# Both normalisations of the mixing stage on ScalarE, with a shift from GpSimd, in place of VectorE

## The chip, the core and the metric

The kernel runs on one core of a Trainium2 chip. The metric is the device time of one execution in microseconds (us). The engines are PE (TensorE: PE is its matmuls, PEld its weight loads), DVE (VectorE), ACT (ScalarE), POOL (GpSimd) and SP (SyncE, which issues DMAs). They run their own instruction streams and meet at semaphores.

## The reference

One transformer-like block over 8 batches of 512 tokens with 256 features, all in float32; a class row is put ahead of each batch.

```python
h = _L0_tok_ref(x, w_qkv, b_qkv, w_out, b_out)            # attention, 16 heads
h = concatenate([broadcast(cls_tok), h], axis=1)           # 513 rows
h = h + _L0_attn_ref(_layernorm(h), a_params, B_w, C_w, D) # linear recurrence over the tokens, + D * u
h = h + _L0_ffn_ref(_layernorm(h), ...)                    # shared expert + top 2 of 8 experts

def _layernorm(x, axis=-1, eps=1e-05):
    m = jnp.mean(x, axis=axis, keepdims=True)
    v = jnp.var(x, axis=axis, keepdims=True)
    return (x - m) / jnp.sqrt(v + eps)
```

The two calls of `_layernorm` are what the change is about. In the recurrence's input they give `u`, in the experts' input `u2`.

## The kernel before

The program has three stages. The first makes queries, keys and values and runs attention for all batches (to about 505 us of the span). The second, `stage_mix`, which this case is about, takes the batches one by one. The third (from about 790 us) runs tiles of 128 token rows through the experts that were chosen.

A batch is four tiles (TT = 4) of 128 tokens on the partitions by 256 features. The mixing stage has nine steps, b = 0 to 8, written out by hand (`batches`, which calls each engine's `step`). Step b carries batch b through the recurrence (`this`), batch b-1 through the shared expert (`prev`), and batch b+1 through its output projection and first normalisation (`nxt`). What an engine does, in what order, is fixed by the order of the calls in its `step`; only semaphores (`ev[...]`) couple the engines.

Around the change one batch goes so:

- PE turns (transposes) the second-normalised rows `u2` (`turn_rows`, L1210), ACT copies the result to `u2_short`, DVE makes the rest (`cut_second`), ACT copies `u2_T`, PE makes the router's logits (L1347) and the first part of the shared expert's products (L73). Meanwhile PE projects the next batch's heads, and DVE adds the bias and takes the statistics (`first_sum`: `sum_and_statistics`, L1429 to L1437).
- POOL raises variance + eps of the four tiles to the power -1/2 (`inverse_deviation`, L1069). DVE makes `u` of the next batch: `normalise`, L1443, four instructions, (row - mean) * inverse deviation. DVE adds the router's bias (L1560), ACT takes the sigmoid (L1187), DVE chooses two experts (L854 to L1501) and multiplies the shared expert's gates (L1415).
- PE turns `u`, ACT copies the result to `u_T` behind a silu (L1132, L1136), PE makes the state's input (`make_state`, L1243), DVE turns and scans it (`turn_back`, L1477 on; `make_hidden`), PE makes `y` (L1255).
- POOL computes d * u + h (L1081, L1084) as soon as `u` is there and the choice of the batch before is made.
- DVE adds `y` and takes the second statistics, POOL the power, DVE places the rows' slots (`place`, L1460 to L1466), makes `u2` (L1443 again) and adds the shared expert's result (L1420). Meanwhile PE runs `shared_down` (L1281). POOL issues eight indirect DMAs of slots a batch (L1103); the next batch's power stands behind the sixth.

In steps 1 to 5 ACT also rounds one early weight (L891) and DVE subtracts it (`cut_weights`, L899), between the gates and `turn_back`. In batch 0 the attention stage's code makes `u` (`beside`), and in step 0 DVE carries the class rows as well.

ACT keeps one set of function tables at a time. Sigmoid and silu lie in different sets, so an ACT_TABLE_LOAD stands ahead of each of the two; the plain copies need none.

Of the kernel before, what the change touches and what calls it, by code (L numbers as in the profile page):

```python
# [23 lines left out]
FP32 = mybir.dt.float32  # L24
# [3 lines left out]
ALU = mybir.AluOpType  # L28
ACT = mybir.ActivationFunctionType
# [891 lines left out]
def stage_mix(nc, mem, dram):  # L921

    ident = mem["ident"]
    with ExitStack() as ctx:
# [22 lines left out]
        w_s_rest, w_s = mem["w_s_rest"], (mem["wg_s"], mem["wu_s"])  # L947
        stats = sb("mix_stats", [P, TT, 6], FP32)
        mv = sb("mix_mv", [P, TT, 2], FP32)
        rstd = sb("mix_rstd", [P, TT], FP32)  # L950
        probs = sb("mix_probs", [P, TT, E], FP32)
        for name, shape in (("counts", [P, E]), ("need", [P, E]), ("ends", [P, E]), ("tile_f", [P, 2, TILES])):
            mem[name] = sb(name, shape, FP32)
# [111 lines left out]
        @block.gpsimd  # L1065
        def _(pool):
            def inverse_deviation(b, which):
                pool.wait_ge(ev[f"stats{which}"], b + 1)
                pool.tensor_tensor(rstd[:, :], mv[:, :, 1], mem["minus_half"][:, 0:TT], ALU.pow).then_inc(ev[f"pow{which}"], 1)  # L1069

            def step(b, par, prev, this, nxt):
                if this:
# [55 lines left out]
        def _(act):  # L1128
# [9 lines left out]
            def class_copy(n, to, bank):  # L1138

                act.wait_ge(ev["cls_turned"], n + 1)  # L1140
                act.activation(to, cls_ps[bank][:, 0:D].rearrange("p (c n) -> p c n", c=2), ACT.Copy).then_inc(ev["cls_copied"], 1)

            def step(b, par, prev, this, nxt):
                if this and prev:
                    copy_turned(u_T, b, "u_turned", "uT_copied")
# [26 lines left out]
                if last:  # L1172
                    act.wait_ge(ev["y_made"], 2 * B)
                    for n in (10, 11, 12):
                        shorten_weights(act, mem, n)
                if last:
                    copy_turned(u2_T, b, "u2_turned", "u2T_copied")
                    act.wait_ge(ev["u2T_copied"], b + 1)
                    act.activation(short(u2_short[:, :, :]), u2_T[:, :, :], ACT.Copy).then_inc(ev["shared_shortened"], 1)
                elif this:  # L1180
                    copy_turned(short(u2_short), b, "u2_turned", "shared_shortened")

                    act.wait_ge(ev["u2_cut"], b + 1)
                    copy_turned(u2_T, b, "u2_turned", "u2T_copied")
                if this:
                    act.wait_ge(ev["logits_biased"], b + 1)
                    act.activation(probs[:, :, :], probs[:, :, :], ACT.Sigmoid).then_inc(ev["sigmoid"], 1)  # L1187
                    silu(b, 0)
# [222 lines left out]
        def _(dve):  # L1411
# [11 lines left out]
            def sum_and_statistics(b, rows, term, which, link):  # L1423

                product, done = (("out_made", "h_done"), ("y_made", "h2_done"))[which - 1]
                for n in range(2):
                    dve.wait_ge(ev[product], 2 * b + n + 1)
                    pair = rows[:, 2 * n:2 * n + 2, :]
                    dve.tensor_tensor(pair, made[:, n, :].rearrange("p (t n) -> p t n", t=2),  # L1429
                                      pair if term is None else term, ALU.add).then_inc(ev[done], 1)  # L1430
                    dve.wait_ge(ev[done], 2 * b + n + 1)
                    for t in (2 * n, 2 * n + 1):
                        link(dve.bn_stats(stats[:, t, :], rows[:, t, :]), wait=(t == TT - 1))  # L1433
                dve.sem_inc(ev["stats_ready"])
                for t in range(TT):
                    link(dve.bn_aggr(mv[:, t, :], stats[:, t, :]), wait=(t == TT - 1))
                dve.tensor_scalar(mv[:, :, 1], mv[:, :, 1], EPS, None, ALU.add).then_inc(ev[f"stats{which}"], 1)  # L1437

            def normalise(b, rows, which):
                dve.wait_ge(ev[f"pow{which}"], b + 1)  # L1440
                to = (u, u2)[which - 1]
                for t in range(TT):
                    last = dve.tensor_scalar(to[:, t, :], rows[:, t, :], mv[:, t, 0:1], rstd[:, t:t + 1],  # L1443
                                             ALU.subtract, ALU.mult)
                last.then_inc(ev["u_done" if which == 1 else "u2_done"], 1)

            def cut_second(b):
                dve.wait_ge(ev["shared_shortened"], 2 + b + 1)
# [47 lines left out]
            def step(b, par, prev, this, nxt):  # L1496
# [32 lines left out]
                    class_act()  # L1529
                elif nxt:  # L1530
                    place(b - 1, 1 - par)
                if this:
                    dve.wait_ge(ev["u2_turned"], b)
                    dve.wait_ge(ev["u2_stored"], 16 * b)
                    normalise(b, h2[:, par, :, :], 2)
                if this and not nxt:
                    place(b - 1, 1 - par)
                if prev:
# [13 lines left out]
                    first_sum(b + 1)  # L1552
                if not prev:
                    class_add()
                if nxt:
                    dve.wait_ge(ev["u_turned"], b + 1)
                    normalise(b + 1, h, 1)
                if this:
                    dve.wait_ge(ev["logits_made"], b + 1)
                    dve.tensor_tensor(probs[:, :, :], turn[:, 0, 0:TT * E].rearrange("p (t e) -> p t e", e=E),  # L1560
# [38 lines left out]
            def beside(g, n):  # L1599
# [8 lines left out]
                if (g, n) == (2, 0):  # L1608
                    copy_turned(heads_T, "heads_turned", "hT_copied")
                    class_state()  # L1610
                    first_sum(0)
                elif (g, n) == (2, 1):
                    normalise(0, h, 1)
                elif (g, n) == (3, 0):
                    copy_turned(u_T, "u_turned", "uT_copied")
                    class_end()
                    turn_back(0, scan)
                elif (g, n) == (3, 1):
                    make_hidden(0, scan)
# [519 lines left out]
```

## Time and profile before

| | us |
|---|---|
| median of 3 runs | 1169.42 (1168.76 to 1169.72) |
| the profiled execution | 1169.99 |
| its span | 1168.3 |
| PE busy | 1112.9 (95%) |
| DVE busy | 916.5 (78%) |
| ACT busy | 584.5 (50%) |
| POOL busy | 401.2 (34%) |

The span runs from the first to the last instruction that the profiler saw; the execution's time is a little longer. The busy shares are means over all three stages. In the mixing stage batches 1 to 6 follow each other in steady steps of about 34.95 us. In a timeline row stand the start and the length in us, engine, line, operation, the tile written <- the tiles read, and in brackets how long the engine had been idle and what ended that.

### The profile page before, as it was taken

The numbers are of one execution on the slowest core, as the hardware profiler recorded it, in microseconds if no ns is written. First come the engines' busy times: TensorE is split into PE (matmuls) and PEld (weight loads), VectorE is DVE, ScalarE is ACT, GpSimd is POOL, SyncE is SP. The second block draws the span as 40 slices with busy tenths as digits, with TensorE's granted clock in tenths as the row PEclk, the third lists the DMA queues.
The fourth block names the chain that finished last, engine by engine and source line by source line (L and its number), as shares of the span: only waits on it lengthen the run. The fifth ranks groups of instructions, "written<-read, shape, count | busy, mean of one in ns | idle before, by whom it ended". The sixth has DMA issues, their size and how long they took to land.

```text
span 1168.3 us, 22138 instructions
## 1 busy us (share of the span) xinstructions
PE 1112.9 (95%) x6022; PEld 713.9 (61%) x6023; DVE 916.5 (78%) x1567; ACT 584.5 (50%) x973; POOL 401.2 (34%) x516
## 2 busy tenths in 40 slices
PE   6998999999999999989999999977999999999996
PEld 3654333333333333477777777766888888888885
DVE  3788888888888888678888888786777777777775
ACT  3544777777777777641332322532444444444442
POOL 3011630101011111203455343453555555545553
PEclk9998999999999999999999999988999999999998
DMA  8786232323323332041345431222333333333332
GB/s 290 262 259 220 67 110 70 107 72 103 94 82 97 95 83 70 19 142 39 91 109 109 92 81 52 48 57 63 58 50 53 52 55 54 54 54 54 54 55 33
DMA packets 108691, 105.38 MB, mean 90 GB/s; under 512 B 42464, under 2 KB 97904, under 8 KB 108624
## 3 DMA queue, kind: packets, MB, share of 16 engines
q1 hardware_dynamic: 90528, 81.18, 24.3%
q0 software_dynamic: 18112, 23.57, 11.6%
q8 instruction: 25, 0.41, 0.2%
q14 instruction: 26, 0.21, 0.1%
HBM read 64.88 MB, written 39.68 MB: 89 GB/s over the span
## 4 chain that ended last, share of the span: by engine, by line
PE 70%; DVE 10%; POOL 5%; issue 4%; DMA 1%; ACT 1%; POOLq 0%; DVEq 0%; SPq 0%; ACTq 0%
PE mix_pairs L73 20%; PE pv L673 11%; PE by_key L662 10%; PE by_query L653 9%; PE mix_made L1821 9%; POOL kept_table L1103 4%; PE mix_turn L1808 3%; PE mix_made L1255 2%; PE mix_made L1243 2%; PE by_query L694 2%; PE mix_turn L1788 1%; DVE mix_stats L1433 1%; DVE k_mix_u L1443 1%; DVE mix_h L1429 1%; DVE mix_back L1486 1%
## 5 line engine op out<-in xcount | busy, mean ns | idle before, releaser
L747 DVE TENSOR_REDUCE k_neg_max<-by_query 128x2 f32<-128x1024 f32 x240 | 282.8, 1220 | 49.0 <-PE by_query L653 46.2
L807 ACT ACTIVATE k_wu_e<-by_key 128x512 f32<-128x512 f32 x512 | 270.2, 600 | 65.5 <-PE by_key L662 65.4
L662 PE MATMUL by_key<-k_wg_e 99*128 99x512 bf16 x512 | 175.2, 384 | 3.4 <-DVE pv L783 3.0
L1765 POOL DMA_INDIRECT out_rows<-x_y,k_slot x72 | 114.0, 1583 | 158.3 <-PE mix_turn L1788 111.6
L653 PE MATMUL by_query<-k_wg_e 96*128 96x512 bf16 x480 | 144.7, 382 | 0.0
L1863 ACT ACTIVATE x_gate<-mix_pairs 128x512 f32<-128x512 f32 x72 | 43.0, 597 | 200.8 <-PE mix_pairs L73 200.8
L673 PE MATMUL pv<-k_wu_e,k_wd_e 128*17 128x512 f32 x1024 | 134.6, 598 | 0.2 <-ACT k_wu_e L807 0.2
L73 PE MATMUL mix_pairs<-w_short,x_T 128*128 x288 | 121.7, 423 | 2.1 <-issue 2.1
L1821 PEld LDWEIGHTS mix_made<-x_wd,x_acts_T 128*128 128x128 f32 x864 | 111.2, 188 | 7.4 <-ACT x_acts_T L1886 0.9
L73 PE MATMUL mix_pairs<-w_short,x_rest 128*128 x288 | 114.6, 398 | 0.0
L1821 PE MATMUL mix_made<-x_wd,x_acts_T 128*128 128x256 f32 x864 | 112.6, 279 | 0.7 <-ACT x_acts_T L1886 0.7
L1928 DVE TENSOR_TENSOR x_wd<-k_wd_e,x_wd 128x1024 fp32r<-128x1024 f32 x72 | 88.3, 1227 | 18.2 <-issue 16.9
L662 PEld LDWEIGHTS by_key<-k_wg_e 99*128 99x128 bf16 x512 | 43.6, 97 | 93.2 <-ACT k_wu_e L807 55.0
L128 POOL CAST k_max_parts<-k_neg_max 128x16 bf16<-128x16 f32 x32 | 6.4, 201 | 226.4 <-DVE k_neg_max L747 129.2
L1875 ACT ACTIVATE x_wd<-k_wd_e 128x1024 fp32r x72 | 76.4, 1062 | 12.9 <-PE mix_pairs L1281 6.9
L653 PEld LDWEIGHTS by_query<-k_wg_e 96*128 96x128 bf16 x480 | 46.8, 98 | 58.9 <-DVE k_wd_e L761 7.0
L915 POOL DMA_INDIRECT k_x_in<-kept_x_rows,k_slot x72 | 73.3, 1019 | 27.3 <-issue 21.3
L1906 DVE CAST x_T<-mix_turn 128x256 fp32r<-128x256 f32 x72 | 30.6, 425 | 66.5 <-PE mix_turn L1788 64.7
L1103 POOL DMA_INDIRECT kept_table<-k_pay,k_slot_i x64 | 66.9, 1045 | 37.0 <-DVE k_slot_i L1466 20.6
L309 PE MATMUL qk_ps<-k_wu_e,k_wqkv 128*128 128x512 f32 x128 | 60.4, 614 | 10.0 <-DMA k_wu_e<-in_xT 10.0
L73 PEld LDWEIGHTS mix_pairs<-w_short,x_rest 128*128 128x128 f32 x288 | 54.6, 190 | 13.2
L73 PE MATMUL mix_pairs<-u_short,w_s_short 128*128 128x512 f32 x128 | 57.7, 450 | 3.6 <-DVE mix_gate L1415 2.7
(244 smaller groups left out, 1950.3 us busy)
## 6 DMA issues: line engine op xcount, KB each, us to landing
k_wg_e<-kept_qk SPq DMA_DIRECT2D x384, 64.0 KB, 2.1
kept_qk<-k_qk_parts SPq DMA_DIRECT2D x32, 384.0 KB, 3.1
kept_v<-k_v_ones SPq DMA_DIRECT2D x8, 544.0 KB, 5.1
k_wd_e<-kept_v SPq DMA_DIRECT2D x32, 136.0 KB, 2.7
k_wu_e<-in_xT POOLq DMA_DIRECT2D x8, 512.0 KB, 5.9
kept_heads<-k_wd_e SPq DMA_DIRECT2D x8, 512.0 KB, 3.0
k_heads_in<-kept_heads SPq DMA_DIRECT2D x8, 512.0 KB, 10.2
k_wg_e<-in_wg_e SPq DMA_DIRECT2D x8, 512.0 KB, 7.6
```

The source lines that it names most:

```text
L73: mm = pe.matmul(out, short(lhs[a]), short(rhs[b]), start=(start and n == 0), stop=(stop and n == 2))
L653: pe.matmul(by_query[:, pair_bank(b, g, k // 2) + k % 2, :], q_rows[0:KROWS, g, h, t * P:(t + 1) * P], k_rows[0:KROWS, g, h, :], start=Tru ...
L662: pe.matmul(by_key[:, key_bank(job), :], k_rows[0:SROWS, g, h, kt * P:(kt + 1) * P], q_rows[0:SROWS, g, h, :], start=True, stop=True).then ...
L673: mm = pe.matmul(pv[PV_ROWS * h:PV_ROWS * h + VW, :], v_unit[:, g, kt, h, :], probs[:, G * (kt // 2) + h, kt % 2, :], start=(kt == 0), sto ...
L747: dve.tensor_reduce(neg_max[:, g % 2, 2 * n:2 * n + 2], by_query[:, bank:bank + 2, :], AX.X, ALU.max, negate=True).then_inc(query_read, 1)
L807: act.activation(probs[:, key_tile(j) // 2 * G + j // 2 % G, j % 2, :], by_key[:, key_bank(job), :], ACT.Exp, scale=float(HD) ** -0.5).the ...
L915: pool.indirect_dma_start(out=mem["x_in"][:, r % FIRST_X, :], out_offset=None, in_=dram["x_rows"], in_offset=bass.IndirectOffsetOnAxis(ap= ...
L1103: pool.indirect_dma_start(out=dram["table"], in_offset=None, in_=mem["pay"][:, 1 - par, t, n, :], out_offset=bass.IndirectOffsetOnAxis(ap= ...
L1765: pool.indirect_dma_start(out=dram["out"], in_=y[:, r % 2, :], in_offset=None, compute_op=ALU.add, out_offset=bass.IndirectOffsetOnAxis(ap ...
L1821: mm = pe.matmul(ps_y[:, r % 2, 0:D], short(acts_T[:, a, m, :]), short(wd[:, par, b, m, :]), start=(n == 0 and m == 0), stop=(n == 2 and m ...
L1875: act.activation(short(wd[:, r % 2, 0, :, :]), mem["wd_e"][:, bass.ds(e, 1), :, :].rearrange("p e m n -> p (e m) n"), ACT.Copy).then_inc(e ...
L1928: dve.tensor_tensor(short(wd[:, r % 2, 1, :, :]), mem["wd_e"][:, bass.ds(e, 1), :, :].rearrange("p e m n -> p (e m) n"), wd[:, r % 2, 0, : ...
```

## The change

`normalise` moves from the DVE program to the ACT program. ACT computes func(scale * in + bias), here with the identity, with the inverse deviation as scale and -mean * inverse deviation as bias, both one number per partition. POOL makes this bias (`shift`) with two more operations behind each power, so the semaphores `pow1` and `pow2` now count three a batch. Further waits guard `rstd`, `shift` and `mv`: POOL waits for the other normalisation (`u_done`, `u2_done`), DVE for the other shift before it overwrites `mv`. Batch 0's `u` is still made by DVE (`normalise_first`).

```diff
@@ gpsimd
             def inverse_deviation(b, which):
                 pool.wait_ge(ev[f"stats{which}"], b + 1)
+                if which == 1:
+                    pool.wait_ge(ev["u2_done"], b)
+                else:
+                    pool.wait_ge(ev["u_done"], b + 1)
                 pool.tensor_tensor(rstd[:, :], mv[:, :, 1], mem["minus_half"][:, 0:TT], ALU.pow).then_inc(ev[f"pow{which}"], 1)
+                pool.wait_ge(ev[f"pow{which}"], 3 * b + 1)
+                pool.tensor_tensor(shift[:, :], mv[:, :, 0], rstd[:, :], ALU.mult).then_inc(ev[f"pow{which}"], 1)
+                pool.wait_ge(ev[f"pow{which}"], 3 * b + 2)
+                pool.tensor_tensor(shift[:, :], mem["zeros"][:, 0:TT], shift[:, :], ALU.subtract).then_inc(ev[f"pow{which}"], 1)
@@ scalar
+            def normalise(b, rows, which):
+                act.wait_ge(ev[f"pow{which}"], 3 * b + 3)
+                to = (u, u2)[which - 1]
+                for t in range(TT):
+                    last = act.activation(to[:, t, :], rows[:, t, :], ACT.Identity, bias=shift[:, t:t + 1],
+                                          scale=rstd[:, t:t + 1])
+                last.then_inc(ev["u_done" if which == 1 else "u2_done"], 1)
@@ scalar, step
+                if this:
+                    act.wait_ge(ev["u2_turned"], b)
+                    act.wait_ge(ev["u2_stored"], 16 * b)
+                    normalise(b, h2[:, par, :, :], 2)
                 if last:
                     copy_turned(u2_T, b, "u2_turned", "u2T_copied")
...
                     copy_turned(u2_T, b, "u2_turned", "u2T_copied")
+                if nxt:
+                    act.wait_ge(ev["u_turned"], b + 1)
+                    normalise(b + 1, h, 1)
                 if this:
                     act.wait_ge(ev["logits_biased"], b + 1)
                     act.activation(probs[:, :, :], probs[:, :, :], ACT.Sigmoid).then_inc(ev["sigmoid"], 1)
@@ vector, sum_and_statistics
+                if which == 2:
+                    dve.wait_ge(ev["pow1"], 3 * b + 3)
+                else:
+                    dve.wait_ge(ev["pow2"], 3 * b)
                 dve.sem_inc(ev["stats_ready"])
@@ vector
-            def normalise(b, rows, which):
-                dve.wait_ge(ev[f"pow{which}"], b + 1)
-                to = (u, u2)[which - 1]
+            def normalise_first():
+                dve.wait_ge(ev["pow1"], 3)
                 for t in range(TT):
-                    last = dve.tensor_scalar(to[:, t, :], rows[:, t, :], mv[:, t, 0:1], rstd[:, t:t + 1],
+                    last = dve.tensor_scalar(u[:, t, :], h[:, t, :], mv[:, t, 0:1], rstd[:, t:t + 1],
                                              ALU.subtract, ALU.mult)
-                last.then_inc(ev["u_done" if which == 1 else "u2_done"], 1)
+                last.then_inc(ev["u_done"], 1)
@@ vector, step: both calls go
-                if this:
-                    dve.wait_ge(ev["u2_turned"], b)
-                    dve.wait_ge(ev["u2_stored"], 16 * b)
-                    normalise(b, h2[:, par, :, :], 2)
...
-                if nxt:
-                    dve.wait_ge(ev["u_turned"], b + 1)
-                    normalise(b + 1, h, 1)
```

ACT's instructions in step 1, from the gate of the third part (L1132) over the two copies of turned `u2` to the copy of turned `u` in the next step, before:

```order
L1132 ACTIVATE mix_gate<-mix_pairs 128x512 [waits mix_down_made,mix_gate_made]
L1136 ACTIVATE u2_short<-mix_turn 128x1024 [waits mix_u2_turned]
L1136 ACTIVATE k_mix_u2_T<-mix_turn 128x1024 [waits mix_u2_turned,mix_u2_cut]
L1187 ACT_TABLE_LOAD
L1187 ACTIVATE mix_probs<-mix_probs 128x32 [waits mix_logits_biased]
L1132 ACT_TABLE_LOAD [waits mix_down_made]
L1132 ACTIVATE mix_gate<-mix_pairs 128x512 [waits mix_gate_made]
L1136 ACTIVATE k_mix_u_T<-mix_turn 128x1024 [waits mix_u_turned]
```

And now (L1156 is `normalise`, L1211 the sigmoid, L1141 the silu, L1145 the copies):

```order
L1141 ACTIVATE mix_gate<-mix_pairs 128x512 [waits mix_down_made,mix_gate_made]
L1156 ACTIVATE k_mix_u2<-mix_h2,mix_shift,mix_rstd 128x256 [waits mix_pow2,mix_u2_stored,mix_u2_turned]
L1156 ACTIVATE k_mix_u2<-mix_h2,mix_shift,mix_rstd 128x256 x3
L1145 ACTIVATE u2_short<-mix_turn 128x1024 [waits mix_u2_turned]
L1145 ACTIVATE k_mix_u2_T<-mix_turn 128x1024 [waits mix_u2_turned,mix_u2_cut]
L1156 ACTIVATE k_mix_u<-k_mix_h,mix_shift,mix_rstd 128x256 [waits mix_pow1,mix_u_turned]
L1156 ACTIVATE k_mix_u<-k_mix_h,mix_shift,mix_rstd 128x256 x3
L1211 ACT_TABLE_LOAD
L1211 ACTIVATE mix_probs<-mix_probs 128x32 [waits mix_logits_biased]
L1141 ACT_TABLE_LOAD [waits mix_down_made]
L1141 ACTIVATE mix_gate<-mix_pairs 128x512 [waits mix_gate_made]
L1145 ACTIVATE k_mix_u_T<-mix_turn 128x1024 [waits mix_u_turned]
```

The second normalisation stands ahead of the copies of `u2`. The first stands between them and the load of the sigmoid's table, which stood right behind the copy before.

POOL's instructions from the second normalisation's power of one batch to the product and sum d * u + h of the next (L1103 is the indirect DMAs of slots), before:

```order
L1069 TENSOR_TENSOR mix_rstd<-mix_mv,k_minus_half 128x4 [waits mix_stats2]
L1103 DMA kept_table<-k_pay,k_slot_i 35072x2 [waits mix_slots_ready]
L1103 DMA kept_table<-k_pay,k_slot_i 35072x2 x5
L1069 TENSOR_TENSOR mix_rstd<-mix_mv,k_minus_half 128x4 [waits mix_stats1]
L1103 DMA kept_table<-k_pay,k_slot_i 35072x2 x2
L1081 TENSOR_TENSOR mix_h2<-k_mix_u,k_d_row 128x1024 [waits acc_stored,mix_cls_stored,mix_chosen_done,mix_u_done]
L1084 TENSOR_TENSOR mix_h2<-mix_h2,k_mix_h 128x1024 [waits mix_ud_done]
```

And now, from the DMAs on (L1074 the power, L1076 and L1078 the shift, L1112 the DMAs, L1090 and L1093 product and sum):

```order
L1112 DMA kept_table<-k_pay,k_slot_i 35072x2 [waits mix_slots_ready]
L1112 DMA kept_table<-k_pay,k_slot_i 35072x2 x5
L1074 TENSOR_TENSOR mix_rstd<-mix_mv,k_minus_half 128x4 [waits mix_u2_done,mix_stats1]
L1076 TENSOR_TENSOR mix_shift<-mix_mv,mix_rstd 128x4 [waits mix_pow1]
L1078 TENSOR_TENSOR mix_shift<-k_zeros,mix_shift 128x4 [waits mix_pow1]
L1112 DMA kept_table<-k_pay,k_slot_i 35072x2 x2
L1090 TENSOR_TENSOR mix_h2<-k_mix_u,k_d_row 128x1024 [waits acc_stored,mix_cls_stored,mix_chosen_done,mix_u_done]
L1093 TENSOR_TENSOR mix_h2<-mix_h2,k_mix_h 128x1024 [waits mix_ud_done]
```

Between the power and the last two DMAs stand the two operations on the shift.

## Rows read from the trace of the kernel before

**Rows 1.** Windows: length; busy us of PE, PEld, DVE, ACT, POOL; clock; DMA share; GB/s.

```profile
594.32:629.26 34.94, 33.82 (x167) 26.81 (x166) 29.73 (x78) 10.12 (x12) 15.63 (x12) 1.00 0.33 93
```

**Rows 2.** Chain of waits, 594 to 605: start us, us, what.

```profile
594.32 1.04 POOL mix_rstd L1069
...
595.46 1.53 DVE k_mix_u L1443 x4
...
597.24 1.06 PE mix_turn L1210 x8
...
604.56 0.69 DVE k_x_in L1477
```

**Rows 3.** Timeline of ACT: start us, us, line, operation, tiles, idle before, releaser.

```profile
591.80 1.28 ACT L1187 ACT_TABLE_LOAD   x1
597.12 0.23 ACT L1187 ACTIVATE mix_probs<-mix_probs 128x32 f32<-128x32 f32 x1 [4.04 <-DVE mix_probs L1560]
597.37 1.28 ACT L1132 ACT_TABLE_LOAD   x1
598.67 0.60 ACT L1132 ACTIVATE mix_gate<-mix_pairs 128x512 f32<-128x512 f32 x1
599.16 1.02 ACT L1136 ACTIVATE k_mix_u_T<-mix_turn 128x1024 f32<-128x1024 f32 x1
```

**Rows 4.** Timeline of DVE in the same stretch.

```profile
597.39 0.19 DVE L854 TENSOR_REDUCE k_best<-mix_probs 128x4 f32<-128x32 f32 x1 [0.30 <-ACT mix_probs L1187]
...
600.50 0.19 DVE L1501 TENSOR_TENSOR mix_chosen<-k_hot 128x32 bf16<-128x32 f32 x1
...
602.70 1.58 DVE L899 TENSOR_TENSOR wg_rest<-k_wg_e,w_short 128x1024 fp32r<-128x1024 f32 x1 [0.26 <-ACT w_short L891]
```

**Rows 5.** Timeline of POOL in the same stretch.

```profile
600.84 2.36 POOL L1081 TENSOR_TENSOR mix_h<-k_mix_u,k_d_row 128x1024 f32<-128x1024 f32 x1 [2.98 <-issue]
603.28 3.26 POOL L1084 TENSOR_TENSOR mix_h<-mix_h,k_mix_h 128x1024 f32<-128x1024 f32 x1
```

**Rows 6.** Timeline of PE in the same stretch.

```profile
600.93 3.60 PE L1243 MATMUL mix_made<-k_mix_u_T,k_m_T 128*128 128x512 f32 x8
```

**Rows 7.** Instruction groups of ACT by shape: count, busy us, mean ns, idle before.

```profile
L355 ACT ACTIVATE k_qk_parts<-qk_ps,k_bqk 128x512 bf16<-128x512 f32 x32 | 22.0, 687 | 37.0 <-PE qk_ps L309 36.1 <-DMA kept_qk<-k_qk_parts 0.9
...
L1132 ACT ACTIVATE mix_gate<-mix_pairs 128x512 f32<-128x512 f32 x32 | 19.1, 598 | 65.9 <-PE mix_pairs L73 65.8
...
L891 ACT ACTIVATE w_short<-k_wg_e 128x1024 fp32r<-128x1024 f32 x8 | 8.4, 1049 | 4.3 <-PE mix_made L1255 4.3
...
L1141 ACT ACTIVATE mix_gate<-mix_pairs 128x256 f32<-128x256 f32 x1 | 0.4, 374 | 0.0
```

**Rows 8.** The same view for POOL, smallest two-input operation.

```profile
L470 POOL TENSOR_TENSOR k_wd_e<-k_power 128x2 f32<-128x2 f32 x9 | 1.8, 195 | 0.7
```

**Rows 9.** Timeline of POOL at the second normalisation's power.

```profile
583.55 1.04 POOL L1069 TENSOR_TENSOR mix_rstd<-mix_mv,k_minus_half 128x4 f32<-128x4 f32 x1 [11.96 <-DVE mix_mv L1437]
```

**Rows 10.** Timeline of PEld up to the turning of u2.

```profile
582.84 4.29 PEld L1281 LDWEIGHTS mix_pairs<-k_wd_s,mix_gate 128*128 128x128 f32 x20
587.26 0.80 PEld L1210 LDWEIGHTS mix_turn<-k_ident,k_mix_u 128*128 128x128 f32 x7
```

**Rows 11.** Timeline of PE, batches 0 and 1.

```profile
520.91 1.94 PE L1210 MATMUL mix_turn<-k_ident,k_mix_u 128*128 128x128 f32 x8 [1.47 <-DVE mix_probs L1560]
...
527.32 3.60 PE L1243 MATMUL mix_made<-k_mix_u_T,k_m_T 128*128 128x512 f32 x8
...
540.28 5.41 PE L1255 MATMUL mix_made<-k_m_T,k_mix_u_T 128*128 128x256 f32 x16 [2.80 <-DVE k_mix_u_T L1491]
```

**Rows 12.** Timeline of DVE, step 1, weight cut.

```profile
530.79 2.50 DVE L899 TENSOR_TENSOR wg_rest<-k_wg_e,w_short 128x1024 fp32r<-128x1024 f32 x1
```

**Rows 13.** Windows of 1 us after PE's idle time before 540.28.

```profile
541.00:542.00 1.00, 1.00 (x3) 0.78 (x3) 0.96 (x2) 0.00 (x0) 0.00 (x0) 0.50 0.00 0
```

**Rows 14.** Windows of 1 us in an idle time of PE.

```profile
785.00:786.00 1.00, 0.00 (x0) 0.00 (x0) 1.00 (x3) 1.00 (x2) 0.97 (x1) 1.00 1.08 70
```

More of the change, by code:

```diff
@@ L949, in stage_mix @@
         mv = sb("mix_mv", [P, TT, 2], FP32)
-        rstd = sb("mix_rstd", [P, TT], FP32)
+        rstd, shift = sb("mix_rstd", [P, TT], FP32), sb("mix_shift", [P, TT], FP32)
         probs = sb("mix_probs", [P, TT, E], FP32)
@@ L1612, in beside @@
                 elif (g, n) == (2, 1):
-                    normalise(0, h, 1)
+                    normalise_first()
                 elif (g, n) == (3, 0):
```

## The prediction

> **What bounds the kernel now.** Only the mixing stage is touched, so I read that stage. First the busy time by batch: from the power of one batch to the power of the next pass 34.94 us, in which PE is busy 33.82, VectorE (DVE) 29.73, ScalarE (ACT) 10.12 and GpSimd (POOL) 15.63 [rows 1]. ACT has room, DVE has 5.2 us to spare per batch: neither share tells what a moved instruction costs. For that I read the chain of waits through one batch. It goes POOL (inverse deviation, 1.04 us), DVE (the four first normalisations of the next batch, 1.53 us), PE (turning u), PE (make_state), DVE (turn_back at 604.56) [rows 2]. So the first normalisation lies on the chain. Then I read, engine by engine, what follows it. ACT has loaded the sigmoid's table at 591.80, in idle time; it then waits 4.04 us for the logits, runs the sigmoid at 597.12, loads the table back from 597.37, and at 598.67 and 599.16 come the silu and the copy of u's transpose for which make_state waits [rows 3]. DVE starts the choice of two experts when the sigmoid is done (597.39), has it at 600.50 + 0.19, and cuts a weight at 602.70 [rows 4]. POOL's product u*d starts when the choice is made, at 600.84 [rows 5]. make_state starts on PE at 600.93 [rows 6]; the copy had ended at 599.16 + 1.02 = 600.18, so that path has 0.7 us of slack. Turn_back waits only 604.56 - (602.70 + 1.58) = 0.28 us beyond the cut.
>
> The second normalisation runs beside PE's shared_down: its power starts at 583.55 [rows 9], the weight loads before it end at 582.84 + 4.29 = 587.13 and those that turn u2 start at 587.26 [rows 10]. Speeding it up can give 0.13 us a batch and no more.
>
> **The instructions, one by one.** Removed from DVE: 15 groups of four (8 second normalisations, 7 first ones; batch 0's first stays). Added to POOL: a product and a subtraction of 128x4 behind each of the 16 powers. The nearest small two-input operation takes 0.195 us, with 0.7/9 = 0.08 us ahead of each [rows 8]: 2 x 0.28 = 0.56 us. From below nothing bounds it but 2 x 0.195 = 0.39; from above the 128x4 power itself, 1.04 each [rows 9]. I take 0.56, since a product and a subtraction are what the nearer row is.
>
> Added to ACT: four ACTIVATEs of 128x256 with two per-partition operands. The trace has 128x256 without any at 0.374 us; a source in SBUF (0.03: 1.049 in group 7 against 1.02 in group 3) is added, and one per-partition operand costs 0.687 - 0.598 = 0.09 [rows 3, 7]. Two are not shown; between 0 (they ride along: 0.40 each) and something over twice 0.09, I take twice: 0.58 us. ACT's neighbours overlap by 0.11 (0.60 at 598.67, the next at 599.16), so four take 3 x 0.47 + 0.58 = 2.0 us, against 1.53 on DVE; the low end is 3 x 0.29 + 0.40 = 1.3. The Trainium skill ("ScalarE: Activation LUTs", What ACT_TABLE_LOAD costs) says that each such pointer operand adds some 93 ns; our trace shows it for one, and for two it would give the same 2.0 us.
>
> **First normalisation, new times on the old clock.** The power ends at 595.36. With 0.56 on POOL and 0.10 to hand over (595.36 to 595.46 before) ACT starts at 596.02 and ends at 598.02, where DVE ended at 596.99: 1.03 later. Turning u started at 597.24 and comes at about 598.1. The larger part comes behind it. In ACT's order the table load for the sigmoid stands now behind the four ACTIVATEs, so it no longer falls into idle time: load 598.04 to 599.32, sigmoid to 599.57, where it ended at 597.35: 2.22 later. That DVE has the biased logits 2.5 us earlier doesn't help. Two paths lead on to turn_back:
> - by ACT and PE: load back to 600.87, silu 600.89, copy from 601.38 to 602.40, make_state about 602.45 in place of 600.93: +1.5;
> - by DVE and POOL: choice and u*d 2.22 later, so u*d runs 603.06 to 605.42. The cut waits for it: before, u*d ended at 603.20 and the cut, 1.58 us long in place of 1.22, ended at 604.28, 1.08 behind it; while it ran, POOL's next operation stretched to 3.26 [rows 4, 5], and in step 1, where the cut began 1.4 us before the end of u*d, it took 2.50 [rows 12]. POOL and DVE take turns there. So the cut ends at 605.42 + 1.08 = 606.50 and turn_back follows: +1.9.
> The Trainium skill ("SBUF — State Buffer", SBUF: two separate sides) has the rule: a DVE operation with two SBUF inputs and a GpSimd operation that reads SBUF exclude each other for their whole length. By that rule the 2.50 us of step 1 agree with the trace; if they only shared bandwidth, the cut would end before the bound by PE, and the shift be 1.5 us.
>
> The cut exists in steps 1 to 5. First normalisations in steps 1 to 4 (for batches 2 to 5) are followed by one: 4 x 1.9 = 7.6. Those of steps 5 and 6 are not: 2 x 1.5 = 3.0. What comes behind turn_back (the scans, make_y, statistics, the slots, POOL's six descriptors, the next power) is a chain in the same order and moves along.
>
> **Step 0** is different: PE waits 1.47 us before it turns u [rows 11], and DVE has class work until turn_back at 530.79 + 2.50 = 533.29 [rows 12], while make_state(1) ends at 527.32 + 3.60 = 530.92 [rows 11]. Nothing hides batch 0's second normalisation, and both of that step grow as above, by some 1.0 to 1.1 us each (0.56 and 2.0 in place of 1.53 or less): PE comes 2.2 late, and the 2.4 us of slack take it. Cost about 0. There is even a gain: PE then idled 2.80 us ahead of make_y(1), and that ran 5.41 us [rows 11] at a granted clock of 0.50, the 1.2 GHz level [rows 13]. With 2.2 us of that idle time filled the clock should stay at 2.4 GHz, where the same columns take 3.6 us (527.32): I book -1.6.
>
> **Second normalisation, batches 1 to 7.** Power 583.55 + 1.04, POOL 0.56, hand-over 0.10, ACT 2.0: 587.25, and PE turned u2 at 587.26. Nothing, or 0.05 a batch. The waits that the change adds on POOL and DVE (u_done, u2_done, pow) are long met when they are reached; behind POOL's two new operations stand two descriptors that have until the choice, 3 us away (2.98 idle before u*d).
>
> **Sum**: 7.6 + 3.0 + 0 - 1.6 = +9.0 us. The profiled execution took 1169.99 us, 1168.3 of it span; the median is 1169.42. So 1178.4 as a median, 1179.0 for an execution like the profiled one. Its own range: 1.3 us on ACT in place of 2.0 gives 6 x 0.7 less (1174.2); no clock credit and 0.1 us more per POOL operation 1181.
>
> **Rivals.**
> 1. ACT as cheap as 1.3 us: 1174.2. For it: 128x256 is 0.374. Against: the 0.09 of one operand. 0.12.
> 2. The clock falls at the new gap. PE idle before turning u grows from 0.6 to 1.4 us. If the 1.2 GHz level is granted, turning, shared_up and make_state take as in step 0: 1.94 us for the turning in place of 1.06, and 6.4 in place of 3.7 up to make_state (520.91 to 527.32; 597.24 to 600.93): 2.7 x 6 = 16 on top, 1195. For it: the clock was at half after 2.80 us of idle time, and in step 0 after 1.47 us that follow the thin logit products [rows 11, 13]. Against: it stayed at 1.00 through a whole idle microsecond at 785 [rows 14], and here full shared_up products stand before the gap. 0.10.
> 3. The table load costs more than its 1.28 us. The trace shows 0.02 us after it [rows 3]. 0.03, time 6 x 1.4 more, 1187. The Trainium skill ("ScalarE: Activation LUTs", the same section) adds a drain of about 1.38 us to each load; the trace doesn't bear it out, since the next ACTIVATE starts 0.02 us behind the load.
> 4. The load isn't late (the sigmoid's path hides it): only turning u moves, by 0.9, the copy's 0.7 of slack takes part of it, and 6 x 0.2 to 0.9 stay: 1171 to 1175, I say 1171. 0.05. The order of ACT speaks against it.
> 5. Faster: DVE is the bound, and the 15 groups with 1.4 us each come off it: -21, 1148. It decides if the place of slots, add and first sum on DVE start earlier without the second normalisation. But these wait for shared_down and for ACT's copy, as PE's 587.13 and 587.26 tell, and the chain has DVE's first normalisation as a stage that ACT now lengthens. 0.04.
> The forecast has 0.66.
>
> A measurement of this kernel tells 0.2% (2.3 us) from no change. Slower by more: 0.66 + 0.12 + 0.10 + 0.03 = 0.91. Same, with rival 4, 0.05; faster 0.04. The range of 8 in 10: 1173.5 to 1184.
>
> **What the profile would show.** The ACTIVATEs at 0.58 and four in 2.0 us; POOL's two operations at 0.2 each; the sigmoid's load right behind the first normalisation; idle time of PE before make_state 0.6 and before turning u 1.4; cuts of 2.0 to 2.5 us in steps 2 to 5; a batch of 36.8 us (steps with a cut) and 36.5, in place of 34.94; make_y(1) near 3.6 us. Wrong would be: batches of 35.2 or less (the load is hidden), of 39 or more (clock), or u2 turned later than 0.1 us behind shared_down.

## The result and the profile after

The changed kernel takes 1178.71 us (1178.29 to 1179.54, 5 runs), the one before 1169.42 us on the same chip: a ratio of 1.0086 (95% interval 1.0074 to 1.0097). (The recorded ratio is a little above the quotient of the two medians, 1.0079, which lies in its interval.) By the medians it is slower by 9.3 us; forecast were 9.0 (1178.4). Its profiled execution has a span of 1177.9 us against 1168.3.

Read it in the order of the prediction. The windows first, from one power to the next, a step with a weight cut and then one without (columns as in [rows 1]; both are of the changed kernel):

```profile
594.97:631.96 36.99, 34.27 (x167) 26.67 (x166) 27.58 (x71) 14.15 (x20) 16.40 (x17) 1.00 0.38 75
705.93:742.72 36.79, 34.26 (x167) 26.66 (x166) 25.30 (x70) 13.21 (x19) 15.50 (x17) 1.00 0.38 73
```

The step grew from 34.94 us [rows 1] to 36.99, although DVE has 2.15 us less to do in it (29.73 to 27.58). ACT has 4.0 us more. Its timeline in the same step answers to [rows 3]:

```profile
596.66 2.07 ACT L1156 ACTIVATE k_mix_u<-k_mix_h,mix_shift,mix_rstd 128x256 f32<-128x256 f32 x4 [4.25 <-POOL mix_shift L1078]
598.75 1.28 ACT L1211 ACT_TABLE_LOAD   x1
600.04 0.23 ACT L1211 ACTIVATE mix_probs<-mix_probs 128x32 f32<-128x32 f32 x1
600.29 1.28 ACT L1141 ACT_TABLE_LOAD   x1
601.59 0.60 ACT L1141 ACTIVATE mix_gate<-mix_pairs 128x512 f32<-128x512 f32 x1
602.08 1.02 ACT L1145 ACTIVATE k_mix_u_T<-mix_turn 128x1024 f32<-128x1024 f32 x1
```

The idle time of 4 us now lies ahead of the normalisation, and the sigmoid's table load behind it: no engine covers it. Before, the order was load, idle time, sigmoid. The four instructions take 2.07 us (forecast 2.0); the groups by tile give one of them 585 ns (forecast 0.58) and a product on POOL 202 ns (forecast 0.20). In these two lines stand the shortest, median and longest time in ns, then the first and the last start.

```profile
L1156 ACT ACTIVATE k_mix_u<-k_mix_h,mix_shift,mix_rstd x28: 584/585/602, 520.9 to 745.9; 128x256 f32<-128x256 f32 x28
...
L1076 POOL TENSOR_TENSOR mix_shift<-mix_mv,mix_rstd x16: 198/202/240, 478.1 to 769.7; 128x4 f32<-128x4 f32 x16
```

PE in the same step. Turning u waits 1.47 us (0.56 before), make_state another 0.48 us for the copy of turned u, where it had not waited at all [rows 6]:

```profile
598.79 1.09 PE L1234 MATMUL mix_turn<-k_ident,k_mix_u 128*128 128x128 f32 x8 [1.47 <-ACT k_mix_u L1156]
603.15 3.70 PE L1267 MATMUL mix_made<-k_mix_u_T,k_m_T 128*128 128x512 f32 x8 [0.48 <-ACT k_mix_u_T L1145]
```

DVE, which answers to [rows 4], and POOL, to [rows 5]:

```profile
600.31 0.19 DVE L854 TENSOR_REDUCE k_best<-mix_probs 128x4 f32<-128x32 f32 x1 [5.33 <-ACT mix_probs L1211]
...
604.73 2.46 DVE L899 TENSOR_TENSOR wg_rest<-k_wg_e,w_short 128x1024 fp32r<-128x1024 f32 x1
607.12 0.68 DVE L1505 TENSOR_TENSOR k_x_in<-mix_made,k_cos 128x512 f32<-128x512 f32 x1
```

```profile
603.75 2.35 POOL L1090 TENSOR_TENSOR mix_h<-k_mix_u,k_d_row 128x1024 f32<-128x1024 f32 x1 [4.33 <-issue]
606.18 3.27 POOL L1093 TENSOR_TENSOR mix_h<-mix_h,k_mix_h 128x1024 f32<-128x1024 f32 x1
```

DVE idles 5.33 us for the sigmoid. Then its cut begins at 604.73 while POOL's product runs until 603.75 + 2.35 = 606.10, and takes 2.46 us in place of 1.58: it ends 1.09 us behind the product, as before. Turn_back follows it without a gap. In steps 6 and 7, which have no cut, turn_back waits for make_state.

The second normalisation, from PE's weight loads (answers to [rows 10]): the loads of shared_down end at 582.90 + 4.72 = 587.62, and PE waits 0.32 us.

```profile
582.90 4.72 PEld L1305 LDWEIGHTS mix_pairs<-k_wd_s,mix_gate 128*128 128x128 f32 x22
587.94 0.86 PEld L1234 LDWEIGHTS mix_turn<-k_ident,k_mix_u 128*128 128x128 f32 x8 [0.32 <-ACT k_mix_u L1156]
```

In step 0 PE turns u of batch 1 at 523.00, 2.1 us later than before, but make_state of batch 1 comes at 528.30 and is only 1.0 us later ([rows 11] has 520.91 and 527.32). The 1.1 us between lie in the clock: from 523.00 to 526.20 it is granted at 0.50 and rises then, where before the change it stood at 0.50 from 520 to past 526.

```profile
523.00 1.97 PE L1234 MATMUL mix_turn<-k_ident,k_mix_u 128*128 128x128 f32 x8 [2.53 <-ACT k_mix_u L1156]
528.30 3.60 PE L1267 MATMUL mix_made<-k_mix_u_T,k_m_T 128*128 128x512 f32 x8
```

And batch 1's y, [rows 11]: 3.92 us in place of 5.41, behind 1.74 us of idle time in place of 2.80. The idle time is 1.06 us shorter, as make_state came 1.0 us later.

```profile
540.20 3.92 PE L1279 MATMUL mix_made<-k_m_T,k_mix_u_T 128*128 128x256 f32 x16 [1.74 <-DVE k_mix_u_T L1519]
```

The start of turn_back in each step shows where the time came in (us, both traces; the last column is what the step added):

| step | before | after | shift | added |
|---|---|---|---|---|
| 1 | 533.21 | 533.12 | -0.1 | |
| 2 | 569.62 | 570.12 | +0.5 | +0.6 |
| 3 | 604.56 | 607.12 | +2.6 | +2.1 |
| 4 | 639.52 | 644.11 | +4.6 | +2.0 |
| 5 | 674.47 | 681.09 | +6.6 | +2.0 |
| 6 | 709.42 | 717.86 | +8.4 | +1.8 |
| 7 | 744.38 | 754.64 | +10.3 | +1.8 |

Step 2's 0.6 is the 2.05 of a step with a cut less 1.5 of batch 1's y. Behind step 7 the shift stays at 10.25 us on PE (the last part of the shared expert starts at 791.49 against 781.24). Then the first gather of the expert stage comes at 804.94 against 796.35 (+8.6), and the span ends +9.6. The gather waits for the slots. Of the last eight slot descriptors two took 2.03 and 1.96 us before, and 0.96 each now. First before:

```profile
786.35 2.03 POOL L1103 DMA_INDIRECT kept_table<-k_pay,k_slot_i  x1 [0.30 <-issue]
788.68 1.96 POOL L1103 DMA_INDIRECT kept_table<-k_pay,k_slot_i  x1 [0.30 <-issue]
```

```profile
786.31 1.22 DVE L899 TENSOR_TENSOR wg_rest<-k_wg_e,w_short 128x1024 fp32r<-128x1024 f32 x1
```

And after:

```profile
796.51 0.96 POOL L1112 DMA_INDIRECT kept_table<-k_pay,k_slot_i  x1 [0.30 <-issue]
797.77 0.96 POOL L1112 DMA_INDIRECT kept_table<-k_pay,k_slot_i  x1 [0.30 <-issue]
```

```profile
796.63 1.21 DVE L899 TENSOR_TENSOR wg_rest<-k_wg_e,w_short 128x1024 fp32r<-128x1024 f32 x1
```

Before, a descriptor began 0.04 us behind the start of a cut on DVE; now it begins 0.12 us ahead of one. So the slots are done at 798.73 against 790.64, 8.1 us later instead of 10.25. No term of the prediction had this; it hangs on how the two queues happen to meet. The 0.5 us from there to the gather and the 1.0 us that the expert stage adds were not followed up.

### The profile page after: what moved, and what is told of

Same layout as the page of the kernel before. It is cut to its first block, busy times and chain, and to the rows that moved or that the text cites. A ratio compares the mean times of both kernels' runs of the same rounds, so it can differ in the third digit from the quotient of the medians.

```text
span 1177.9 us, 22186 instructions
## 1 busy us (share of the span) xinstructions
PE 1113.7 (95%) x6022; PEld 711.2 (60%) x6023; DVE 898.1 (76%) x1507; ACT 614.6 (52%) x1033; POOL 403.9 (34%) x548
## 4 chain that ended last, share of the span: by engine, by line
PE 72%; DVE 9%; ACT 3%; issue 3%; POOL 2%; DMA 1%; POOLq 0%; DVEq 0%; ACTq 0%; SPq 0%
PE mix_pairs L73 18%; PE pv L673 11%; PE by_key L662 10%; PE by_query L653 9%; PE mix_made L1842 8%; PE mix_pairs L1305 4%; PE mix_turn L1829 3%; PE mix_made L1279 3%; PE by_query L694 2%; PE mix_turn L1809 1%; ACT k_mix_u L1156 1%; PE mix_made L1267 1%; DVE mix_stats L1457 1%; DVE mix_back L1514 1%; PE mix_turn L1234 1%
## 5 line engine op out<-in xcount | busy, mean ns | idle before, releaser
L1112 POOL DMA_INDIRECT kept_table<-k_pay,k_slot_i x64 | 64.0, 1001 | 35.1 <-issue 18.6
L73 PEld LDWEIGHTS mix_pairs<-w_short,x_T 128*128 128x128 f32 x288 | 55.0, 191 | 10.1 <-issue 3.3
```

What stands on the lines that cost most here:

```text
L73: mm = pe.matmul(out, short(lhs[a]), short(rhs[b]), start=(start and n == 0), stop=(stop and n == 2))
L1112: pool.indirect_dma_start(out=dram["table"], in_offset=None, in_=mem["pay"][:, 1 - par, t, n, :], out_offset=bass.IndirectOffsetOnAxis(ap= ...
```

## The experiments

The theory that the runs test: the first normalisation alone carries the cost, by three terms on one path (0.56 us on POOL, 0.5 on ACT, the table load of 1.28), with the cut behind POOL's product on top. The rivals: a share for the second normalisation; only the longer way to u, not the table load; and for batch 1's gain, relief of an engine rather than the clock. Times are medians; each ratio is to the kernel before on the same chip, with its 95% interval. The median of the kernel before was 1169.31 us for e1 to e4, 1169.10 for e5 to e8 and 1170.70 for e9 and e10.

**e1, the first normalisation alone on ACT.**

```diff
                 pool.tensor_tensor(rstd[:, :], mv[:, :, 1], ..., ALU.pow).then_inc(ev[f"pow{which}"], 1)
+                if which == 1:
+                    ... # the two operations on shift
-                if this:
-                    ...
-                    normalise(b, h2[:, par, :, :], 2)          # ACT
+                if this:
+                    ...
+                    normalise_rows(u2, h2[:, par, :, :], "u2_done")  # DVE, behind place
```

> Only the first normalisation is on ScalarE; the second is back on VectorE, and GpSimd makes a shift for the first alone. Theory: the first carries the cost (about 2.0 us a batch with a weight cut, 1.8 without), the second costs 0.1 us a batch and 1 us in step 0. So 1178 us, and 1179.5 if the idle time of PE ahead of batch 1's y, now longer again, lets the clock fall. Rival: both normalisations carry a share each (ScalarE needs 2.07 us for four in place of 1.4 to 1.5, GpSimd 0.56 us more, twice a batch): then about 1174.

1177.62 us, ratio 1.0072 (1.0059 to 1.0086): the theory's number. Steps with a cut are 36.8 us, but for one of 37.2 (36.99 with both), so the second costs 0.17 us a step, and 1.1 in all. Batch 1's y took 3.92 us, behind 0.68 us of idle time: the clock stayed up here too.

**e2, the second alone.** The same edit the other way round.

> Only the second normalisation is on ScalarE; the first is back on VectorE behind the power alone. Theory: hidden by shared_down, 0.1 us a batch and 1.1 us in step 0 that class work takes; 1169.5 us (1168.0 to 1170.5, the low end if the clock stays up in batch 1). Rival, both carry a share: 1174. Rival, VectorE is the bound and 8 x 1.4 us come off it: 1158.

1171.33 us, ratio 1.0019 (1.0010 to 1.0028), 1.8 us above the forecast 1169.5. Steady steps of 35.1 us (+0.15) are as expected, and VectorE is not the bound: eight normalisations less on it made nothing faster. The step-0 part was wrong: turn_back of batch 1 comes at 534.68, 1.5 us later than before. With the first normalisation on DVE the class work starts only behind it (522.16 against 520.67 before), so the later start is not absorbed. In the changed kernel that normalisation has left DVE and the class work starts at 520.62; this is what made room. Batch 1's y was slow here (a granted clock of 0.50), behind 3.11 us of idle time.

**e3, the sigmoid ahead of the first normalisation.**

```diff
+                if this:
+                    act.wait_ge(ev["logits_biased"], b + 1)
+                    act.activation(probs..., ACT.Sigmoid).then_inc(ev["sigmoid"], 1)
                 if nxt:
                     act.wait_ge(ev["u_turned"], b + 1)
                     normalise(b + 1, h, 1)
                 if this:
-                    act.wait_ge(ev["logits_biased"], b + 1)
-                    act.activation(probs..., ACT.Sigmoid).then_inc(ev["sigmoid"], 1)
                     silu(b, 0)
```

> The changed kernel with one move: ScalarE takes the sigmoid (its table is loaded in idle time again) ahead of the first normalisation, and the silu's table load stands behind it. Theory: the late table load is the larger part. The choice on VectorE and u*d on GpSimd no longer wait for it, the copy of turned u comes one load earlier, and what stays is the turning of u 0.9 us later and some 0.25 behind it: 6 x 1.15 less 1.5 of the clock in batch 1 less 0.7 at the end, 1174.3 us. Rival, ScalarE's and GpSimd's longer time to u is all of it: 1178.7, no change. The sigmoid starts 3.9 us behind the power's stage in the changed kernel and should start ahead of it.

1173.11 us, ratio 1.0029 (1.0020 to 1.0039): 5.6 us of the 9.3 go with the place of the sigmoid and its table load in ACT's order. ACT's timeline:

```profile
592.92 1.28 ACT L1208 ACT_TABLE_LOAD   x1
595.50 0.23 ACT L1208 ACTIVATE mix_probs<-mix_probs 128x32 f32<-128x32 f32 x1 [1.30 <-DVE mix_probs L1582]
597.15 2.07 ACT L1156 ACTIVATE k_mix_u<-k_mix_h,mix_shift,mix_rstd 128x256 f32<-128x256 f32 x4 [1.42 <-POOL mix_shift L1078]
599.24 1.28 ACT L1141 ACT_TABLE_LOAD   x1
601.03 1.02 ACT L1145 ACTIVATE k_mix_u_T<-mix_turn 128x1024 f32<-128x1024 f32 x1
```

The load and the sigmoid lie in the wait for u's power. Steps are 36.05 us (expected 34.95 + 1.15 = 36.1). The cuts take 1.23 us in place of 2.46, because the choice on DVE starts 0.3 us behind the power in place of 5.3 and POOL's product has ended before the cut begins; turn_back then waits for make_state. The profiled execution is the slowest of ten, which spread from 1170.1 to 1176.2; in it batch 1's y ran 5.41 us.

**e4, no shift as operand.** `act.activation(to, rows, ACT.Copy, scale=rstd)` in place of Identity with a bias; the function changes with the operand.

> The changed kernel without the shift as operand: ScalarE multiplies by the inverse deviation only, the mean is not subtracted (GpSimd still computes the shift, and ScalarE still waits for it). Theory: each per-partition operand adds 0.09 us; four instructions of 0.49 in 1.7 us in place of 0.585 in 2.07; 6 x 0.38 less: 1176.4 us. Rival, the second operand costs nothing beside the first: 0.58 each and 1178.7.

1175.80 us, ratio 1.0055 (1.0041 to 1.0068). One instruction has a mean of 496 ns against 589 (medians 492 and 585) (columns: sum in us, mean in ns, idle time ahead and what ended it):

```profile
L1156 ACT ACTIVATE k_mix_u<-k_mix_h,mix_rstd 128x256 f32<-128x256 f32 x28 | 11.9, 496 | 29.7 <-POOL mix_shift L1078 29.7
```

So Identity with the second operand costs 93 ns more, as much as the first operand was taken for; that Copy and Identity cost the same by themselves was not tested. The steps are 36.5 us, 0.5 less than 36.99 for 4 x 0.09 = 0.36; the rest is the second normalisation, which no longer makes PE wait (u2 is turned right behind shared_down).

**e5, both normalisations of step 0 on DVE.** ACT's `normalise` calls get `and prev`; DVE makes u2 of batch 0 and u of batch 1 itself.

> The changed kernel, but both normalisations of step 0 stay on VectorE; ScalarE has them from step 1 on. Theory: the 1.5 us that batch 1 gained came from PE, which reached batch 1's y with less idle time and so at the 2.4 GHz level (3.92 us in place of 5.41). Here the idle time is 2.8 us as before the change, the y of batch 1 should take over 5 us at half the granted clock, and the time be 1178.7 + 1.5 = 1180.2 us. Rival: batch 1's gain came from ScalarE or VectorE being relieved in step 1, which is kept here: 1178.7.

1181.39 us, ratio 1.0101 (1.0086 to 1.0117): 2.7 us above the changed kernel (expected 1.5), with less of the change in it. Batch 1's y:

```profile
541.11 5.11 PE L1279 MATMUL mix_made<-k_m_T,k_mix_u_T 128*128 128x256 f32 x16 [3.11 <-DVE k_mix_u_T L1525]
```

The idle time is back and the slow y with it. Relief of an engine in step 1, kept here, is not the gain. The 1.2 us beyond the expectation: step 2 to 3 took 37.3 us here and turn_back of batch 1 came at 534.04; the cause of these was not followed up.

**e6, the cut moved.**

```diff
-                if 1 <= b <= EARLY:
-                    cut_weights(dve, mem, b - 1)
                 if this and prev:
                     turn_back(b, scan)
...
                     shared_add(b - 1, 1 - par, 0)
+                    if b <= EARLY:
+                        cut_weights(dve, mem, b - 1)
```

> The changed kernel, with VectorE's early weight cut of steps 1 to 5 moved from ahead of turn_back to between the two adds of the shared expert's result, where VectorE waits for PE anyway. Theory: the cut waited for GpSimd's u*d (2.46 us for 1.22) and bounded turn_back. Now every step should grow as the ones without a cut, by 1.8 in place of 2.05 us (4 x 0.23 less), and batch 1's turn_back come when make_state is done, up to 1.2 us earlier: 1176.6 us (1177.8 without the latter). Cuts of 1.22 us. Rival: PE's path bounds anyway: 1178.7.

1181.08 us, ratio 1.0096 (1.0080 to 1.0111): slower where the theory said faster. The cuts do take 1.22 us and batch 1's turn_back does come 1.3 us earlier (531.79). But three steps took 38.1 us, two 37.2, and the last, which has no cut, 36.8 (36.99 and 36.79 in the changed kernel). POOL's, DVE's and PE's timelines in one of the slow ones:

```profile
586.95 1.83 POOL L1112 DMA_INDIRECT kept_table<-k_pay,k_slot_i  x1 [1.53 <-DVE k_slot_i L1494]
```

```profile
586.63 1.22 DVE L899 TENSOR_TENSOR wu_rest<-k_wu_e,w_short 128x1024 fp32r<-128x1024 f32 x1
```

```profile
598.94 1.93 PE L1234 MATMUL mix_turn<-k_ident,k_mix_u 128*128 128x128 f32 x8 [1.91 <-ACT k_mix_u L1156]
```

The cut now runs beside POOL's first slot descriptor, which begins 0.32 us behind the cut's start and takes 1.83 us in place of 1.05. It is the first of six ahead of the next power. POOL used to idle 0.36 us ahead of that power, so the power comes 0.44 us later against PE, and PE idles 1.91 us ahead of turning u in place of 1.47. In three of the five steps with a cut the turning is slow too, 1.93 us here in place of 1.09. The windows of that stretch (the clock stands third from the end):

```profile
598.00:599.00 1.00, 0.06 (x1) 0.06 (x2) 0.00 (x0) 0.98 (x3) 0.69 (x2) 1.00 1.14 359
599.00:600.00 1.00, 1.00 (x5) 1.00 (x6) 0.00 (x0) 1.00 (x1) 0.58 (x1) 0.51 1.91 136
```

The granted clock falls to half, the 1.2 GHz level, after the idle time. That is the prediction's rival 2. But in the next step the idle time is the same and the clock stays up:

```profile
637.04 1.09 PE L1234 MATMUL mix_turn<-k_ident,k_mix_u 128*128 128x128 f32 x8 [1.92 <-ACT k_mix_u L1156]
```

```profile
637.00:638.00 1.00, 0.96 (x9) 0.96 (x10) 0.00 (x0) 0.99 (x1) 0.69 (x1) 1.00 1.69 91
```

The three slow steps are those of 38.1 us, the two at the full clock those of 37.2. So one fall of the clock cost about 0.85 us a step, and the stretched descriptor took back what the shorter cut gave. Idle times of 1.91 to 1.93 us gave both levels; what decides between them is open.

**e7, the kernel before with the router's bias ahead of the first normalisation on DVE.** The two blocks change places.

> The kernel before with one move: VectorE adds the router's bias while it waits for GpSimd's power, ahead of the first normalisation. Theory: PE turns u 0.19 us earlier a batch (it waited for the biased logits last), 6 x 0.19: 1168.2 us against 1169.3, at the edge of what can be measured. Rival: the sigmoid and its path bound, and they now start 2.4 us earlier: then up to 0.4 us a batch, 1166.9.

1168.02 us, ratio 0.9988 (0.9979 to 0.9997). Steps of 34.8 us. This is the expected 1.1 us (1169.10 less 1168.02), at the edge of the measurable.

**e8, combined:** e2's split, e7's order, e6's cut, and `class_choose(); class_place()` right behind `class_act()` in step 0.

> A version made from what the theory says: the second normalisation alone on ScalarE; the router's bias ahead of the first normalisation on VectorE; the weight cut between the two adds; and the class rows' choice and slots, 5.7 us of VectorE's work in step 0, moved into its idle time ahead of batch 0's cut of u2. Theory: step 0 loses its VectorE bound (turn_back of batch 1 about 2 us earlier), steady steps of 34.9 us: 1166.5 us, and 1165 if the clock stays up in batch 1. Rival: the 5.7 us delay u2's cut and step 0 gives nothing: 1169.5.

1167.35 us, ratio 0.9984 (0.9975 to 0.9993). Batch 1's turn_back came at 529.38, 3.8 us earlier than before, but steps with a cut took 35.35 us (one 35.7) and the one without 34.94, in place of e7's 34.8: the first descriptor takes 1.82 us here too. Batch 1's y ran in 3.93 us, a further gain. Of all this 2.9 us were left at the turn_back of batch 7 and 1.75 in the median, 0.85 us short of the forecast 1166.5: the longer steps of the moved cut and of the second normalisation on ACT gave back 2.4 us of some 5.3 by then. What was lost behind that point was not followed up.

**e9, no operations on the shift.** POOL's two operations go, ACT takes `bias=mv[:, t, 0:1]`.

> The changed kernel without GpSimd's product and subtraction; ScalarE takes the mean itself as its second operand (so the wrong shift is added), with the same four instructions. Theory: GpSimd's 0.56 us lie on the path of the first normalisation in full: turning u, make_state and the cut each 0.56 us earlier in 6 steps, 3.4 us less: 1175.3 us. Rival: the late table load and what hangs on it set the time whatever comes before it, or PE's idle time takes it: 1178.7.

1175.44 us, ratio 1.0042 (1.0029 to 1.0056): 3.3 us less than the changed kernel, expected 3.4. But this chip was slower; against the kernel before on it the loss is 4.7 us in place of 9.3, which makes 4.6 us less. The steps agree with the larger number: 36.30 us with a cut in place of 36.99, 0.69 less. 0.56 of that are POOL's two operations (PE idles 0.92 us ahead of turning u in place of 1.47), and the rest is the second normalisation, which no longer makes PE wait. POOL's half microsecond is on the path in full.

**e10, all on DVE, better ordered.**

```diff
+                if not prev:
+                    class_choose()
                 if this:
                     cut_second(b)
                 if nxt:
                     first_sum(b + 1)
...
-                if nxt:
-                    dve.wait_ge(ev["u_turned"], b + 1)
-                    normalise(b + 1, h, 1)
                 if this:
                     ... # logits_biased
+                if nxt:
+                    dve.wait_ge(ev["u_turned"], b + 1)
+                    normalise(b + 1, h, 1)
                 if not prev:
-                    class_choose()
                     class_place()
```

> Both normalisations on VectorE as before the change. The router's bias stands ahead of the first normalisation (which alone gave about 1 us), the weight cuts stay where they were, and the class rows' choice alone (14 short operations, 2.8 us) moves into VectorE's idle time ahead of batch 0's cut of u2. Theory: step 0 is bound by VectorE's class work; turn_back of batch 1 comes some 1.7 us earlier, PE idles less ahead of its y and keeps the 2.4 GHz level there (3.9 us in place of 5.4), steady steps stay at 34.8 us: 1164.8 us. Rival: the choice delays the cut of u2 by 0.6 us and gives it all back, no gain in step 0: 1168.0.

1166.67 us, ratio 0.9966 (0.9954 to 0.9978): the fastest of all, 4.0 us under the kernel before on that chip (1170.70), where about 4.5 were expected. Turn_back of batch 1 comes at 531.75, 1.5 us earlier. PE in steps 0 and 1:

```profile
522.21 1.97 PE L1210 MATMUL mix_turn<-k_ident,k_mix_u 128*128 128x128 f32 x8 [1.57 <-DVE k_mix_u L1443]
...
538.83 3.92 PE L1255 MATMUL mix_made<-k_m_T,k_mix_u_T 128*128 128x256 f32 x16 [1.19 <-DVE k_mix_u_T L1491]
```

The y of batch 1 runs in 3.92 us, and steps are 34.8 us but for one of 36.05 in this execution. In that one DVE waits 2.55 us ahead of the router's bias in place of 1.05, though the logits are done in time; no row names the cause.

## Why the prediction was right

- **The chain.** It read that the first normalisation lies on the chain and the second beside shared_down. e1 against the changed kernel gives the second 1.1 us of 9.3.
- **The instructions.** 0.58, 2.0 and 0.20 were forecast, 0.585, 2.07 and 0.20 measured. Whether a second operand costs as much as the first was the open end of that term; e4, which changes the function with it, has 93 ns for it.
- **The late table load.** Forecast: the sigmoid ends 2.22 us later relative to the power (597.35 - 594.32 = 3.03 before). Measured: 600.27 - 594.97 = 5.30, so 2.27 later. e3 took the load out of the path and 5.6 us with it. Rival 4 (the load hidden) is out.
- **The two paths.** 1.5 and 1.9 us a step were forecast, 1.82 and 2.03 measured. Of this 0.14 to 0.17 is the second normalisation (booked as 0 to 0.05; PE's 0.32 us wait). In steps without a cut 0.1 more is that make_state takes 3.70 us in place of 3.60 once it waits for the copy. From the power to turn_back alone a step with a cut grew by 1.91: the cut's path was sized right. Its mechanism, DVE and POOL taking turns, is shown by 2.46 us beside the product, 1.23 in e3, and the descriptor of 1.83 in e6.
- **Step 0.** Turn_back of batch 1 at -0.1 (forecast 0). The explanation lacked a part that e2 showed: the slack was there because the first normalisation left DVE's queue ahead of the class work.
- **The clock's gain.** -1.6 forecast, about -1.5 measured; e5 lost it again by bringing the idle time back. The way there was only half right: 2.2 us of PE's idle time were to be filled, and 1.06 were, because PE's clock in step 0 had risen sooner and make_state came only 1.0 us later. That the y ran fast all the same was partly luck. Over the traces it took 3.92 or 3.93 us behind 0.28 to 1.19 us of idle time (e1, e4, e6, e8, e9, e10) and ran at half the clock behind 2.80 to 3.12 (the kernel before, e2, e5, e7). Between them both came: the fast form behind 1.74 us in the changed kernel, the slow one behind 1.70 in e3. What decides there is open.
- **The sum.** Terms came out 1.3 us higher at step 7 (10.3 for 9.0), the last slot descriptors gave some 2 back, and the expert stage added 1.0; neither was forecast. The hit within 0.3 us owes something to that.
- **Rivals.** ACT at 1.3 us is out (four took 2.07). The clock fell nowhere in the changed kernel's profiled steady steps (rival 2), but in e6 it fell in three of five steps at 0.44 us more idle time, so that rival was near. The table load takes 1.28 us and the next instruction starts 0.01 behind it (rival 3 out). DVE is not the bound (e2).

## What to carry to other kernels

An engine with idle time is not free at every point of its queue: look at what stands there in the idle time, a table load for instance, and put the new work behind it. Had the four instructions stood behind the sigmoid, as in e3, 5.6 of the 9.3 us would not have been lost. And an operation on the chain should not move to an engine that takes longer for it, whatever the busy shares say: 0.5 us more on each of POOL and ACT reached the end, and 2.2 us a step taken from DVE gained nothing in the steady steps.

## What the runs showed of the hardware

- An ACTIVATE of 128x256 takes 374 ns plain with its source in PSUM, 492 with one per-partition operand and its source in SBUF (e4), 585 with two (medians).
- A small operation on POOL has its price by kind: the power of 128x4 takes 1.04 us, the product of the same shape 0.20.
- A DVE operation with two SBUF inputs and POOL's work take turns. A cut that began under POOL's product took 2.46 us in place of 1.22. An indirect DMA's descriptor that began 0.04 to 0.32 us behind the start of a cut took 1.8 to 2.0 us and ended 0.8 to 0.9 behind that cut (e6, and the kernel before at 786.35); one that began 0.12 us ahead of a cut took 0.96 (the changed kernel at 796.51).
- PE's granted clock behind idle time, with full products ahead of it: 1.0 after 1.47 us in all steady steps of the changed kernel, and after 1.91 to 1.93 us in e6 half in three steps and full in two. Behind thin work (products of 8 to 40 columns) both levels were seen too: ahead of turning u in step 0 half after 1.47 us in the kernel before, and ahead of batch 1's y half after 1.70 (e3) and full after 1.74 us.
